# A two-layer decoder on one core: token choice by fused comparisons, and one table for the experts' results

## The chip, the cores and the metric

The kernel runs on one core of one Trainium2 chip. The time is that of one execution on the device, in microseconds (us); the kernel before was run three times. The engines of the core run their own instruction streams and wait for each other through semaphores: TensorE (PE; its weight loads are PEld), VectorE (DVE), ScalarE (ACT), GpSimd (POOL) and SyncE (SP), which issues most transfers.

## The reference

Six sublayers work on x of 8 x 256 tokens with 512 features, each followed by a layer norm of x plus its result: sparse attention, a recurrence, a mixture of experts, causal attention, cross attention and a feed-forward layer. The change touches the choice of tokens in the first, and how results come together in the third.

```python
importance = (x @ Wi + bi)[..., 0]
sorted_desc = jnp.sort(importance, axis=-1)[:, ::-1]
tidx = min(max(1, int(S * SPARSITY_THRESHOLD)), S - 1)      # 51 of 256
sparse_mask = (importance > sorted_desc[:, tidx][:, None]).astype(x.dtype)
_, top_idx = jax.lax.top_k(importance, min(MIN_TOKENS, S))  # 32
min_mask = jnp.zeros_like(importance).at[rows, top_idx].set(1.0)
sparse_mask = jnp.maximum(sparse_mask, min_mask)            # masks k and v
...
probs = jax.nn.softmax(x @ gate_w.T, axis=-1)               # 16 experts
vals, idx = jax.lax.top_k(probs, K)                         # K = 4
w = vals / jnp.sum(vals, axis=-1, keepdims=True)
combine = jnp.einsum('tke,tk->te', jax.nn.one_hot(idx, E, dtype=x.dtype), w)
act = swiglu(jnp.einsum('th,ehi->eti', x, w_gu))
y_e = jnp.einsum('eti,eih->eth', act, w_d)
out = jnp.einsum('te,eth->th', combine, y_e)
out = out + swiglu(x @ w_shared_gate_up) @ w_shared_down
x = _layernorm(x + out, axis=-1)
```

## The kernel before

The residual x stays on the chip for the whole program, as `g.xt` (the trace's `residual`): features on the partitions, 4 x 128 of them, and 2048 tokens in the free dimension. The work is cut into stages, each an `nc.Block()`; between two blocks all engines meet at a barrier, so no engine begins a stage before the last one has ended the stage ahead of it. Inside a stage the order on each engine is that of the code, and semaphores tie the engines together. The helper `Chain` (called `step`) puts a semaphore wait behind an instruction.

Token choice (`sparse_select`, lines 314 to 340). TensorE writes the importance of all tokens to every partition, ScalarE copies it to `imp`. A partition stands for token i of each half batch; `own` is that token's importance for the 16 half batches. VectorE compares all 256 importances of the batch with `own`, once with "at least" (`ge`) and once with "more" (`gt`), sums both, and counts the ties that stand earlier by the table `tri`. `n_ge` decides the threshold, `n_gt` plus the earlier ties is the token's place among the kept ones. From both comes the selection matrix `sel`, with which TensorE gathers the chosen tokens (line 377 on).

Mixture. `route` finds each token's four experts and gives every pair of token and expert a slot in tiles of 256 slots of one expert; a tile is two halves of 128. It writes the tokens' rows, scaled by 64 and split in two 16-bit parts, to the table `token_rows` in HBM, and the scaled rows in 32 bits to the second of two tables `mixed_rows`. Slots without a token point to spare rows behind the 2048 (the constant `spare`, lines 97 and 1067). `experts` runs 8 tiles of the shared expert, whose results SyncE stores into the first table (line 1210), and then 47 tiles of routed ones. For these GpSimd gathers the rows by index (line 1240) and scatters each tile's results with an addition in HBM (line 1252), the first half of a tile into the first table and the second half into the second, so that the residual is already in the sum. A tile's scatter waits until both of the tile before it have landed:

```python
def scatter(j):
    u = j % 2
    wait_out(pool, j - 1)
```

`combine` loads both tables in groups of four blocks of 128 tokens, VectorE adds them, TensorE turns each block by four transposes into one of four PSUM tiles, and ScalarE writes it back to the residual, divided by 64. Layer norm 2 follows (`layer_norm`, line 154 its first matmuls).

Of the kernel before, what the change touches and what calls it, by code (L numbers as in the profile page):

```python
# [17 lines left out]
P = 128  # L18
# [34 lines left out]
           ("choose", 17 * 17), ("spare", 1), ("half16", 2), ("nib_shift", 1)]  # L53
# [13 lines left out]
def constants():  # L67
# [29 lines left out]
    put("spare", T + 1 + p[:, None])  # L97
# [135 lines left out]
def sparse_select(nc, g, a):  # L233


    with ExitStack() as ctx:
# [15 lines left out]
        ge = sb("ge", [P, B, 2, S])  # L252
        gt = sb("gt", [P, B, 2, S])
# [55 lines left out]
        def _(dve):  # L309
# [3 lines left out]
            dve.tensor_copy(wib[:, :, :], bc(wi[:, :], 2, [P, C, P])).then_inc(wib_ready, 1)  # L313
            dve.wait_ge(imp_copied, NT)
# [4 lines left out]
            own_v = own[:, :].rearrange("p (b q) -> p b q", q=2)  # L319
            for q in range(2):  # L320
                mine = bc(own_v[:, :, q], 2, [P, B, S])
                dve.tensor_tensor(ge[:, :, q, :], imp[:, :, :], mine, ALU.is_ge)
                last = dve.tensor_tensor(gt[:, :, q, :], imp[:, :, :], mine, ALU.is_gt)
            step(last)
            n_ge, n_gt, ties, keep = (small[:, k, :] for k in range(4))
            dve.tensor_reduce(n_ge, ge[:, :, :, :].rearrange("p b q j -> p (b q) j"), AX.X, ALU.add)
            step(dve.tensor_reduce(n_gt, gt[:, :, :, :].rearrange("p b q j -> p (b q) j"), AX.X, ALU.add))

            step(dve.tensor_tensor(ge[:, :, :, :], ge[:, :, :, :], gt[:, :, :, :], ALU.subtract))
            step(dve.tensor_tensor(ge[:, :, :, :].rearrange("p b q j -> p b (q j)"),  # L330
                                   ge[:, :, :, :].rearrange("p b q j -> p b (q j)"),
                                   bc(g.const("tri"), 1, [P, B, 2 * S]), ALU.mult))
            step(dve.tensor_reduce(ties, ge[:, :, :, :].rearrange("p b q j -> p (b q) j"), AX.X, ALU.add))
            step(dve.tensor_tensor(ties, ties, n_gt, ALU.add))
# [533 lines left out]
def route(nc, g, a):  # L868
# [3 lines left out]
    with ExitStack() as ctx:  # L872
# [45 lines left out]
        def _(sp):  # L918
# [4 lines left out]
            sp.dma_start(g.rows_dram[T:T + P, :], a["one_row"][:, 0:ROW].to_broadcast([P, ROW])).then_inc(stored, 16)  # L923
            for part in g.sum_dram:
                sp.dma_start(part[T:T + P, :], a["one_row"][:, 0:D].to_broadcast([P, D])).then_inc(stored, 16)
# [536 lines left out]


def combine(nc, g):


    NTOK, GROUP = T // P, 4
    with ExitStack() as ctx:
# [1257 lines left out]
```

## Time and profile before

| | |
|---|---|
| median of 3 runs | 2708.68 us (2708.18 to 2710.73) |
| the profiled execution | 2711.14 us |
| its span | 2709.3 us |
| mean granted TensorE clock | 0.893 |
| token choice on VectorE | 41.98 to 73.07 us |
| combination, first load to last write of the residual | 1410.22 to 1439.55 us |

Times in the rows below are counted from the span's start. "Idle before" is how long the engine stood still ahead of an instruction, with what ended it. The clock is a share of 2.4 GHz. A matmul in 32 bits has more than one record.

### The profile page before, as it was taken

The page shows a single profiled execution, that of the slowest core. Times are in us where ns is not written, and L with a number is a line of the kernel's source. Part 1 is how long each engine was busy: PE and PEld are TensorE (multiplying, and loading weights), DVE is VectorE, ACT ScalarE, POOL GpSimd, SP SyncE. Part 2 cuts the span into 40 slices and gives each one's busy share as a digit, 9 for nine tenths or more (in the row PEclk, how much of TensorE's full clock was granted, in tenths as well). Part 3 has the DMA queues.
Part 4 walks back from the last instruction along what each step waited for, and adds up shares of the span by engine and source line. Part 5 has one row for each costly group of instructions (what it writes and reads, how often), then busy time and mean ns, then how long its engine had stood idle before and what let it go on. Part 6 is the DMA issues. An engine that isn't in the chain of part 4 may idle for free. (4 is left out here: it accounts for less than half of the span.)

```text
span 2709.3 us, 33393 instructions
## 1 busy us (share of the span) xinstructions
PE 2043.6 (75%) x12168; PEld 1270.0 (47%) x12203; DVE 1814.1 (67%) x2409; ACT 1326.7 (49%) x2139; POOL 953.4 (35%) x547
## 2 busy tenths in 40 slices
PE   2788765126498898988956899997994776789986
PEld 1456642012366666666633566663552332344442
DVE  4349883875776777777744356654443897999975
ACT  0013232655376776766734223323553885556656
POOL 1014443213245777777735122224111000443330
PEclk7888887668699999999987999998997998899998
DMA  3224655001637999999964000002334530000001
GB/s 141 62 93 159 241 189 221 0 0 44 235 102 246 254 251 262 247 261 256 251 152 169 0 1 1 1 1 109 92 80 140 187 118 1 0 1 1 1 0 62
DMA packets 123684, 313.63 MB, mean 116 GB/s; under 512 B 29569, under 2 KB 49537, under 8 KB 119810
## 3 DMA queue, kind: packets, MB, share of 16 engines
q1 hardware_dynamic: 102466, 260.69, 27.8%
q0 software_dynamic: 21056, 50.84, 9.5%
q8 instruction: 96, 1.57, 0.2%
q14 instruction: 66, 0.54, 0.1%
HBM read 219.59 MB, written 92.68 MB: 115 GB/s over the span
## 5 line engine op out<-in xcount | busy, mean ns | idle before, releaser
L1406 DVE SCALAR_TENSOR_TENSOR x_part<-x_group,x_scale,x_part 128x256 f32<-128x256 f32 x660 | 287.9, 477 | 144.2 <-ACT x_part L1348 137.5
L1295 PE MATMUL x_group<-x_xt,x_gu 128*128 128x256 f16 x2640 | 346.2, 275 | 2.1 <-ACT x_part L1348 1.2
L1348 ACT ACTIVATE x_part<-x_group,x_scale 128x256 f32<-128x256 f32 x660 | 276.1, 471 | 123.5 <-PE x_group L1295 117.5
L1261 POOL TENSOR_TENSOR x_part<-x_part 128x512 f32<-128x512 f32 x165 | 235.4, 1431 | 196.7 <-DVE x_part L1406 196.7
L1295 PEld LDWEIGHTS x_group<-x_xt,x_gu 128*128 128x128 fp8e4 x2640 | 237.0, 98 | 85.9 <-issue 32.4
L1312 PE MATMUL x_y_ps<-x_d_hi,x_h_hi 128*128 128x512 f32 x330 | 160.0, 485 | 68.8 <-DVE x_h_lo L1419 66.8
L2418 POOL TENSOR_TENSOR f_part<-f_part 128x1024 f32<-128x1024 f32 x44 | 120.4, 2737 | 188.0 <-DVE f_part L2445 188.0
L154 PE MATMUL mean_n<-residual,const_tables 128*128 128x512 f32 x160 | 79.3, 648 | 138.6 <-PEq L733 103.5
L1754 POOL TENSOR_TENSOR c_pt<-c_pt,const_tables 128x1024 f32<-128x1024 f32 x32 | 75.8, 2369 | 258.4 <-ACT c_pt L1728 258.4
L2316 PE MATMUL f_group<-f_x_hi,f_raw 128*128 128x512 f16 x352 | 138.9, 394 | 32.1 <-DVE f_part L2445 24.6
L1252 POOL DMA_INDIRECT mixed_rows<-x_y,moe_rows x94 | 150.1, 1597 | 31.0 <-issue 20.8
L2182 ACT ACTIVATE z_pt<-z_s 128x1024 f32<-128x1024 f32 x128 | 119.7, 1052 | 51.5 <-PE z_s L2153 50.4
L2445 DVE SCALAR_TENSOR_TENSOR f_part<-f_group,f_scale,f_part 128x512 f32<-128x512 f32 x176 | 123.9, 742 | 26.8 <-ACT f_part L2367 21.1
L2316 PE MATMUL f_group<-f_x_lo,f_raw 128*128 128x512 f16 x352 | 138.0, 392 | 0.0
L2367 ACT ACTIVATE f_part<-f_group,f_scale 128x512 f32<-128x512 f32 x176 | 111.0, 679 | 44.2 <-PE f_group L2316 44.0
L1312 PE MATMUL x_y_ps<-x_d_lo,x_h_hi 128*128 128x512 f32 x330 | 131.1, 397 | 0.0
L1312 PE MATMUL x_y_ps<-x_d_hi,x_h_lo 128*128 128x512 f32 x330 | 130.2, 395 | 0.0
L154 PEld LDWEIGHTS mean_n<-residual,const_tables 128*128 128x128 f32 x160 | 32.9, 209 | 181.6 <-issue 181.6
L1240 POOL DMA_INDIRECT x_row<-token_rows,moe_rows x94 | 102.5, 1091 | 21.5 <-issue 16.4
L1312 PEld LDWEIGHTS x_y_ps<-x_d_hi,x_h_hi 128*128 128x128 f32 x330 | 62.5, 189 | 98.0 <-DVE x_h_lo L1419 92.8
L199 ACT ACTIVATE squares_n<-centred_n 128x2048 f32<-128x2048 f32 x24 | 45.9, 1911 | 127.5 <-DVE centred_n L177 127.5
L2330 PE MATMUL f_y<-f_h_hi,f_w_hi 128*128 128x512 f32 x176 | 104.9, 596 | 3.2 <-DVE f_h_lo L2457 2.2
(331 smaller groups left out, 5042.3 us busy)
## 6 DMA issues: line engine op xcount, KB each, us to landing
x_d_hi<-down_hi SPq DMA_DIRECT2D x50, 768.0 KB, 5.7
x_d_lo<-down_lo SPq DMA_DIRECT2D x50, 768.0 KB, 5.9
x_gu<-codes_gu SPq DMA_DIRECT2D x50, 384.0 KB, 5.7
p_w<-d_s SPq DMA_DIRECT2D x17, 768.0 KB, 7.7
down_hi<-p_hi SPq DMA_DIRECT2D x17, 768.0 KB, 3.9
down_lo<-p_lo SPq DMA_DIRECT2D x17, 768.0 KB, 6.3
aux<-ct SPq DMA_DIRECT2D x2, 4096.0 KB, 16.3
cross_values<-y_v_out SPq DMA_DIRECT2D x16, 512.0 KB, 3.0
```

What stands on the lines that cost most here:

```text
L154: mm = pe.matmul(mean_ps[t % 2][:, :], g.const("mean"), tile(src, t)[:, c, :], start=c == 0, stop=c == C - 1)
L1252: pool.indirect_dma_start(out=g.sum_dram[k], out_offset=bass.IndirectOffsetOnAxis(ap=g.rows[:, at:at + 1], axis=0), in_=y[u][:, k, :], in_ ...
L1261: pool.tensor_tensor(x[:, 0, :, :], x[:, 0, :, :], x[:, 1, :, :], ALU.add).then_inc(summed, 1)
L1295: mm = pe.matmul(group_ps[s % 2][:, q, :], codes[:, q, col:col + P], xt[u][:, k, q, :], start=k == 0, stop=k == 1)
L1312: mm = pe.matmul(y_ps[half][:, :], x[u][:, k, rows], w[v][:, k, :], start=k == 0 and i == 0, stop=k == G_I - 1 and i == 2)
L1348: act.activation(part[n % PARTS][:, q, o % 2, :], group_ps[s % 2][:, q, :], ACT.Copy, scale=scale[v][:, o, q:q + 1]).then_inc(ev_act, 1)
L1406: dve.scalar_tensor_tensor(x, group_ps[s % 2][:, 2 + q, :], scale[v][:, o, 2 + q:3 + q], x, ALU.mult, ALU.add).then_inc(ev_dve, 1)
L2182: act.activation(pt[n % RING_P][:, :, :, :], s_ps[n % 3][:, :, :, :], ACT.Exp, scale=HDX ** -0.5)\
L2316: mm = pe.matmul(group_ps[c][:, :], codes[:, n, C * k + c, :], x[t % 2][:, c, :], start=i == 0, stop=i == 1)
L2367: act.activation(part[N % PARTS][:, c, k, :], group_ps[c][:, :], ACT.Copy, scale=scale[:, N % G_F, k, c:c + 1]).then_inc(ev_act, 1)
L2418: pool.tensor_tensor(x[:, 0, :, :], x[:, 0, :, :], x[:, 1, :, :], ALU.add).then_inc(summed, 1)
L2445: dve.scalar_tensor_tensor(x, group_ps[c][:, :], scale[:, N % G_F, k, c:c + 1], x, ALU.mult, ALU.add)\
```

## The change

Token choice: the two long comparisons for each half, the two sums, the subtraction, the multiplication with `tri` and the third sum are replaced by three fused instructions for each of the 16 half batches. Each compares 256 importances with the partition's own one, multiplies by a row of ones, by `tri` (earlier tokens) or by the new table `later` (the others), and writes the sum of the result with `accum_out`. "At least" among the earlier plus "more" among the later is the same place as before. The products go to 16-bit buffers that nothing reads.

Mixture: there is one table `mixed_rows`, with 256 spare rows, 128 for each half of a tile. The scaled rows are no longer stored to HBM. `combine` loads one table in eight groups of two blocks, TensorE waits for the loads directly, and VectorE multiplies the turned block by 1/64 and adds the residual that is on the chip.

VectorE at the token choice, before (`s_small` are the sums, `s_own` the own importances):

```order
L318 TENSOR_REDUCE s_own<-s_sel 128x16
L322 TENSOR_TENSOR s_ge<-s_imp,s_own 128x8x256
L323 TENSOR_TENSOR s_gt<-s_imp,s_own 128x8x256
L322 TENSOR_TENSOR s_ge<-s_imp,s_own 128x8x256
L323 TENSOR_TENSOR s_gt<-s_imp,s_own 128x8x256
L326 TENSOR_REDUCE s_small<-s_ge 128x16
L327 TENSOR_REDUCE s_small<-s_gt 128x16
L329 TENSOR_TENSOR s_ge<-s_ge,s_gt 128x4096
L330 TENSOR_TENSOR s_ge<-s_ge,const_tables 128x4096
L333 TENSOR_REDUCE s_small<-s_ge 128x16
L334 TENSOR_TENSOR s_small<-s_small 128x16
L335 TENSOR_SCALAR s_small<-s_small 128x16
```

and now:

```order
L318 TENSOR_TENSOR s_sel<-s_imp,const_tables 128x2048
L320 TENSOR_REDUCE s_own<-s_sel 128x16
L326 SCALAR_TENSOR_TENSOR s_ge,s_small<-s_imp,s_own,const_tables 128x256
L328 SCALAR_TENSOR_TENSOR s_gt,s_small<-s_imp,s_own,const_tables 128x256
L330 SCALAR_TENSOR_TENSOR s_gt,s_small<-s_imp,s_own,s_later 128x256
...
L330 SCALAR_TENSOR_TENSOR s_gt,s_small<-s_imp,s_own,s_later 128x256
L333 TENSOR_TENSOR s_small<-s_small 128x16
L334 TENSOR_SCALAR s_small<-s_small 128x16
```

Nine instructions over 2048 or 4096 elements have become 48 over 256, three for each of 16 half batches, with no wait from the second to the last.

SyncE's loads in the combination and at the start of the layer norm stage, before (the first two and what follows them; pairs like these stand four times):

```order
L1485 DMA m_mixed<-mixed_rows 128x4x512
L1485 DMA m_kept<-mixed_rows 128x4x512
...
L1468 UNCONDITIONAL_BRANCH
L219 UNCONDITIONAL_BRANCH
L1529 DMA c_rope<-rope 128x1024
L1533 DMA c_wq<-wq 128x2048
```

and now:

```order
L1482 DMA m_mixed<-mixed_rows 128x2x512 x8
L1467 UNCONDITIONAL_BRANCH
L219 UNCONDITIONAL_BRANCH
L1517 DMA c_rope<-rope 128x1024
L1521 DMA c_wq<-wq 128x2048
```

Eight loads of 1 MB, four from each table, have become eight of half the size from one. What follows is the same.

VectorE in the combination and at the start of the layer norm behind it, before:

```order
L1492 TENSOR_TENSOR m_mixed<-m_mixed,m_kept 128x512 x16
L1468 UNCONDITIONAL_BRANCH
L173 UNCONDITIONAL_BRANCH
L177 TENSOR_TENSOR centred_n<-residual,mean_n 128x2048 x3
L190 TENSOR_TENSOR residual<-centred_n,rs_n 128x4x512
```

and now:

```order
L1500 SCALAR_TENSOR_TENSOR residual<-m_turn,residual 128x4x128 x16
L1467 UNCONDITIONAL_BRANCH
L173 UNCONDITIONAL_BRANCH
L177 TENSOR_TENSOR centred_n<-residual,mean_n 128x2048 x3
L190 TENSOR_TENSOR residual<-centred_n,rs_n 128x4x512
```

The additions ahead of the transposes are gone; what ScalarE wrote behind them, VectorE now writes with the residual added.

```diff
@@ the tables of constants
-           ("choose", 17 * 17), ("spare", 1), ("half16", 2), ("nib_shift", 1)]
+           ("choose", 17 * 17), ("spare", HALVES), ("half16", 2), ("nib_shift", 1)]
-    put("spare", T + 1 + p[:, None])
+    put("spare", T + 1 + p[:, None] + P * np.arange(HALVES)[None, :])
@@ sparse_select
-        ge = sb("ge", [P, B, 2, S])
-        gt = sb("gt", [P, B, 2, S])
+        ge = sb("ge", [P, 2 * B, S], F16)
+        gt = sb("gt", [P, 2, 2 * B, S], F16)
+        later = sb("later", [P, 2 * S])
...
+            dve.tensor_scalar(later[:, :], g.const("tri"), -1.0, 1.0, ALU.mult, ALU.add)
             dve.wait_ge(imp_copied, NT)
...
-            own_v = own[:, :].rearrange("p (b q) -> p b q", q=2)
-            for q in range(2):
-                mine = bc(own_v[:, :, q], 2, [P, B, S])
-                dve.tensor_tensor(ge[:, :, q, :], imp[:, :, :], mine, ALU.is_ge)
-                last = dve.tensor_tensor(gt[:, :, q, :], imp[:, :, :], mine, ALU.is_gt)
+            n_ge, ties, after, keep = (small[:, k, :] for k in range(4))
+            ones = g.const("ones")[:, 0:1].to_broadcast([P, S])
+            for n in range(2 * B):
+                b, q, mine = n // 2, n % 2, own[:, n:n + 1]
+                earlier = g.const("tri")[:, q * S:(q + 1) * S]
+                dve.scalar_tensor_tensor(ge[:, n, :], imp[:, b, :], mine, ones, ALU.is_ge, ALU.mult,
+                                         accum_out=n_ge[:, n:n + 1])
+                dve.scalar_tensor_tensor(gt[:, 0, n, :], imp[:, b, :], mine, earlier, ALU.is_ge, ALU.mult,
+                                         accum_out=ties[:, n:n + 1])
+                last = dve.scalar_tensor_tensor(gt[:, 1, n, :], imp[:, b, :], mine, later[:, q * S:(q + 1) * S],
+                                                ALU.is_gt, ALU.mult, accum_out=after[:, n:n + 1])
             step(last)
-            n_ge, n_gt, ties, keep = (small[:, k, :] for k in range(4))
-            dve.tensor_reduce(n_ge, ge[:, :, :, :].rearrange("p b q j -> p (b q) j"), AX.X, ALU.add)
-            step(dve.tensor_reduce(n_gt, gt[:, :, :, :].rearrange("p b q j -> p (b q) j"), AX.X, ALU.add))
-
-            step(dve.tensor_tensor(ge[:, :, :, :], ge[:, :, :, :], gt[:, :, :, :], ALU.subtract))
-            step(dve.tensor_tensor(ge[:, :, :, :].rearrange("p b q j -> p b (q j)"),
-                                   ge[:, :, :, :].rearrange("p b q j -> p b (q j)"),
-                                   bc(g.const("tri"), 1, [P, B, 2 * S]), ALU.mult))
-            step(dve.tensor_reduce(ties, ge[:, :, :, :].rearrange("p b q j -> p (b q) j"), AX.X, ALU.add))
-            step(dve.tensor_tensor(ties, ties, n_gt, ALU.add))
+            step(dve.tensor_tensor(ties, ties, after, ALU.add))
@@ route, SyncE
-            sp.dma_start(g.rows_dram[T:T + P, :], a["one_row"][:, 0:ROW].to_broadcast([P, ROW])).then_inc(stored, 16)
-            for part in g.sum_dram:
-                sp.dma_start(part[T:T + P, :], a["one_row"][:, 0:D].to_broadcast([P, D])).then_inc(stored, 16)
-            kept = g.sum_dram[1][0:T, :].rearrange("(n p) f -> p n f", p=P)
+            for k in range(HALVES):
+                spare = slice(T + k * P, T + (k + 1) * P)
+                sp.dma_start(g.rows_dram[spare, :], a["one_row"][:, 0:ROW].to_broadcast([P, ROW])).then_inc(stored, 16)
+                sp.dma_start(g.sum_dram[spare, :], a["one_row"][:, 0:D].to_broadcast([P, D])).then_inc(stored, 16)
...
-                sp.dma_start(kept[:, n:n + 4, :], scaled[:, n:n + 4, :]).then_inc(stored, 16)
@@ route, VectorE
-            step(dve.tensor_scalar(empty[:, :], row_ps, 0.0, g.const("spare"), ALU.is_equal, ALU.mult))
+            for k in range(HALVES):
+                last = dve.tensor_scalar(empty[:, k::HALVES], row_ps[:, k::HALVES], 0.0, g.const("spare")[:, k:k + 1],
+                                         ALU.is_equal, ALU.mult)
+            step(last)
@@ experts: store() on SyncE, scatter() on GpSimd
-                sp.dma_start(g.sum_dram[0][j * M:(j + 1) * M, :].rearrange("(h p) f -> p h f", p=P), y[u][:, :, :])\
+                sp.dma_start(g.sum_dram[j * M:(j + 1) * M, :].rearrange("(h p) f -> p h f", p=P), y[u][:, :, :])\
...
-                    pool.indirect_dma_start(out=g.sum_dram[k], out_offset=bass.IndirectOffsetOnAxis(ap=g.rows[:, at:at + 1], axis=0),
+                    pool.indirect_dma_start(out=g.sum_dram, out_offset=bass.IndirectOffsetOnAxis(ap=g.rows[:, at:at + 1], axis=0),
@@ combine
-    NTOK, GROUP = T // P, 4
+    NTOK, GROUP = T // P, 2
...
-                for dst, src in ((mixed, g.sum_dram[0]), (kept, g.sum_dram[1])):
-                    rows = src[0:T, :].rearrange("(n p) f -> p n f", p=P)
-                    sp.dma_start(dst[:, part, :], rows[:, part, :]).then_inc(s, 16)
...
-                dve.tensor_tensor(mixed[:, n, :], mixed[:, n, :], kept[:, n, :], ALU.add).then_inc(summed, 1)
+                sp.dma_start(mixed[:, part, :], rows[:, part, :]).then_inc(s, 16)
...
             for n in range(NTOK):
-                pe.wait_ge(summed, n + 1)
+                if n % GROUP == 0:
+                    pe.wait_ge(landed[n // GROUP], 16)
                 if n >= 4:
                     pe.wait_ge(out, n - 3)
...
-        @block.scalar
-        def _(act):
+        @block.vector
+        def _(dve):
             for n in range(NTOK):
-                act.wait_ge(turned, n + 1)
-                act.activation(g.xt[:, :, n * P:(n + 1) * P], turn_ps[n % 4][:, :, :], ACT.Copy, scale=1.0 / X_GAIN)\
-                   .then_inc(out, 1)
+                x = g.xt[:, :, n * P:(n + 1) * P]
+                dve.wait_ge(turned, n + 1)
+                dve.scalar_tensor_tensor(x, turn_ps[n % 4][:, :, :], 1.0 / X_GAIN, x, ALU.mult, ALU.add).then_inc(out, 1)
@@ decoder
-        g.rows_dram = scratch("token_rows", [T + P, ROW])
+        g.rows_dram = scratch("token_rows", [T + HALVES * P, ROW])
-        g.sum_dram = [scratch(f"mixed_rows{k}", [T + P, D]) for k in range(HALVES)]
+        g.sum_dram = scratch("mixed_rows", [T + HALVES * P, D])
```

## Rows read from the trace of the kernel before

**Rows 1.** The page's first part: busy us, share of the span, instructions.
```profile
PE 2043.6 (75%) x12168; PEld 1270.0 (47%) x12203; DVE 1814.1 (67%) x2409; ACT 1326.7 (49%) x2139; POOL 953.4 (35%) x547
```

**Rows 2.** Timeline of VectorE, token choice: start us, us, instruction, idle before and releaser.
```profile
37.34 2.29 DVE L316 TENSOR_TENSOR s_sel<-s_imp,const_tables 128x2048 f32<-128x2048 f32 x1 [17.52 <-ACT s_imp L299]
...
41.98 2.29 DVE L322 TENSOR_TENSOR s_ge<-s_imp,s_own 128x2048 f32<-128x2048 f32 x1
44.19 2.28 DVE L323 TENSOR_TENSOR s_gt<-s_imp,s_own 128x2048 f32<-128x2048 f32 x1
...
50.91 4.42 DVE L326 TENSOR_REDUCE s_small<-s_ge 128x16 f32<-128x4096 f32 x1
...
73.07 0.17 DVE L334 TENSOR_TENSOR s_small<-s_small 128x16 f32<-128x16 f32 x1
73.28 0.17 DVE L335 TENSOR_SCALAR s_small<-s_small 128x16 f32<-128x16 f32 x1
73.36 0.17 DVE L336 TENSOR_SCALAR s_small<-s_small 128x16 f32<-128x16 f32 x1
```

**Rows 3.** Timeline of TensorE where the selection is ready.
```profile
78.44 6.14 PE L377 MATMUL s_row<-s_sel,const_tables 128*128 128x512 f32 x8 [41.86 <-DVE s_sel L340]
```

**Rows 4.** Timeline of the combination stage, all engines.
```profile
1410.22 0.38 SPq L1485 DMA_DIRECT2D m_mixed<-mixed_rows  x1
...
1418.44 2.50 DVE L1492 TENSOR_TENSOR m_mixed<-m_mixed,m_kept 128x512 f32<-128x512 f32 x4 [24.42 <-DMA m_kept<-mixed_rows]
...
1419.19 3.67 PE L1501 MATMUL m_turn<-const_tables,m_mixed 128*128 128x128 f32 x16 [25.95 <-DVE m_mixed L1492]
1420.34 0.60 ACT L1508 ACTIVATE residual<-m_turn 128x512 f32<-128x512 f32 x1 [27.73 <-PE m_turn L1501]
...
1421.19 0.60 ACT L1508 ACTIVATE residual<-m_turn 128x512 f32<-128x512 f32 x1 [0.26 <-PE m_turn L1501]
...
1434.80 2.50 DVE L1492 TENSOR_TENSOR m_mixed<-m_mixed,m_kept 128x512 f32<-128x512 f32 x4 [2.89 <-DMA m_kept<-mixed_rows]
...
1438.41 1.14 ACT L1508 ACTIVATE residual<-m_turn 128x512 f32<-128x512 f32 x2 [0.26 <-PE m_turn L1501]
...
1439.86 7.11 PE L154 MATMUL mean_n<-residual,const_tables 128*128 128x512 f32 x16 [0.94 <-PEq L1468]
```

**Rows 5.** Windows there: busy by engine (instructions), TensorE clock, DMA share, GB/s.
```profile
1418.00:1419.00 1.00, 0.00 (x0) 0.00 (x0) 0.56 (x1) 0.00 (x0) 0.00 (x0) 0.50 1.01 381
```

**Rows 6.** Timeline of the end of the routing stage.
```profile
688.79 1.35 SPq L935 DMA_DIRECT2D token_rows<-r_shares  x1
...
714.70 0.32 DVE L1067 TENSOR_SCALAR r_empty<-r_tok,const_tables 128x94 f32<-128x94 f32 x1 [3.08 <-PE r_tok L965]
```

**Rows 7.** Instructions by line and shape: count, busy us, mean ns, idle before.
```profile
L2445 DVE SCALAR_TENSOR_TENSOR f_part<-f_group,f_scale,f_part 128x512 f32<-128x512 f32 x176 | 123.9, 742 | 26.8 <-ACT f_part L2367 21.1 <-PE f_group L2316 5.2 <-issue 0.2
...
L829 DVE SCALAR_TENSOR_TENSOR w_e<-w_e,w_e_first,w_bb 128x1020 f32<-128x1020 f32 x8 | 10.0, 1250 | 0.0
...
L1009 DVE TENSOR_TENSOR r_p<-r_p,r_m 128x256 f32<-128x256 f32 x1 | 0.4, 426 | 0.0
```

**Rows 8.** Window just after the selection, the same columns as rows 5.
```profile
83.00:84.00 1.00, 1.00 (x4) 0.41 (x3) 0.00 (x0) 0.00 (x0) 0.00 (x0) 0.81 0.00 0
```

**Rows 9.** Timeline of TensorE in the routing stage, four transposes of the residual.
```profile
661.92 0.63 PE L955 MATMUL r_x<-const_tables,residual 128*128 128x128 f32 x4 [0.35 <-ACT r_rows L974]
```

**Rows 10.** Timeline of TensorE at the start of the last layer norm.
```profile
2665.34 9.75 PE L154 MATMUL mean_n<-aux,const_tables 128*128 128x512 f32 x16 [10.10 <-PEq L2483]
```

**Rows 11.** Timeline of GpSimd, scatters of two tiles that follow each other.
```profile
1154.85 1.62 POOL L1252 DMA_INDIRECT mixed_rows<-x_y,moe_rows  x1 [0.15 <-issue]
1156.77 1.57 POOL L1252 DMA_INDIRECT mixed_rows<-x_y,moe_rows  x1 [0.31 <-issue]
...
1166.91 1.63 POOL L1252 DMA_INDIRECT mixed_rows<-x_y,moe_rows  x1 [0.15 <-issue]
```

**Rows 12.** DMA issues between 860 and 1390 us: count, us to landing.
```profile
mixed_rows<-x_y,moe_rows POOLq DMA_INDIRECT x88, 5.4
```

More of the change, by code:

```diff
@@ L932, in _ @@
                   .then_inc(stored, 16)
-                sp.dma_start(kept[:, n:n + 4, :], scaled[:, n:n + 4, :]).then_inc(stored, 16)
             sp.wait_ge(shares_ready, 2)
             sp.dma_start(out[:, :, D:ROW], shares[:, :, :]).then_inc(stored, 16)
-            sp.wait_ge(stored, 16 * (NTOK // 2 + 4))
+            sp.wait_ge(stored, 16 * (NTOK // 4 + 2 * HALVES + 1))
         @block.tensor
@@ L1472, in combine @@
         mixed = ctx.enter_context(nc.sbuf_tensor("m_mixed", [P, NTOK, D], F32))
-        kept = ctx.enter_context(nc.sbuf_tensor("m_kept", [P, NTOK, D], F32))
         turn_ps = [ctx.enter_context(nc.psum_tensor(f"m_turn{i}", [P, C, P], F32)) for i in range(4)]
         landed = [sem(f"landed{i}") for i in range(NTOK // GROUP)]
-        summed, turned, out = sem("summed"), sem("turned"), sem("out")
+        turned, out = sem("turned"), sem("out")
         block = ctx.enter_context(nc.Block())
@@ L1480, in _ @@
         def _(sp):
+            rows = g.sum_dram[0:T, :].rearrange("(n p) f -> p n f", p=P)
             for i, s in enumerate(landed):
                 part = slice(i * GROUP, (i + 1) * GROUP)
-                for dst, src in ((mixed, g.sum_dram[0]), (kept, g.sum_dram[1])):
-                    rows = src[0:T, :].rearrange("(n p) f -> p n f", p=P)
-                    sp.dma_start(dst[:, part, :], rows[:, part, :]).then_inc(s, 16)
-        @block.vector
-        def _(dve):
-            for n in range(NTOK):
-                if n % GROUP == 0:
-                    dve.wait_ge(landed[n // GROUP], 32)
-                dve.tensor_tensor(mixed[:, n, :], mixed[:, n, :], kept[:, n, :], ALU.add).then_inc(summed, 1)
+                sp.dma_start(mixed[:, part, :], rows[:, part, :]).then_inc(s, 16)
         @block.tensor
@@ L1502, in _ @@
                 mm.then_inc(turned, 1)
-        @block.scalar
-        def _(act):
+        @block.vector
+        def _(dve):
             for n in range(NTOK):
-                act.wait_ge(turned, n + 1)
-                act.activation(g.xt[:, :, n * P:(n + 1) * P], turn_ps[n % 4][:, :, :], ACT.Copy, scale=1.0 / X_GAIN)\
-                   .then_inc(out, 1)
-X_RING = 16
+                x = g.xt[:, :, n * P:(n + 1) * P]
+                dve.wait_ge(turned, n + 1)
+                dve.scalar_tensor_tensor(x, turn_ps[n % 4][:, :, :], 1.0 / X_GAIN, x, ALU.mult, ALU.add).then_inc(out, 1)
 def causal_weights(nc, g, a, ctx):
```

## The prediction

> **What bounds the kernel now.** I read the page first: its busy shares [rows 1] say only that no engine is full over the span, and they average over stages that barriers separate. A stage ends when its last engine ends. So a saving on the path inside one stage moves all that follows by the same amount, and one that lies beside that path is worth nothing. I then read the timeline of the stages that the change touches.
>
> Token choice. VectorE works without a gap from 41.98 to 73.07 us: four comparisons over 2048 elements, then five passes over 4096, of which the first stands in the rows [rows 2]. TensorE has nothing to do meanwhile; its next matmul comes after 41.86 us of waiting for the selection [rows 3]. These 73.07 - 41.98 = 31.1 us are all on the path.
>
> Combination of the experts' results. SyncE issues the first load at 1410.22, VectorE starts at 1418.44, its last four additions at 1434.80, when the last load has landed; ScalarE ends at 1438.41 + 1.14 = 1439.55, and the next stage's first matmul is at 1439.86 [rows 4]. Meanwhile the DMA engines move 381 GB/s [rows 5]. The eight loads bring 8 x 128 x 4 x 512 x 4 bytes = 8.39 MB, 22.0 us at that rate; from first issue to last landing it took 24.6, so start and receipt cost 2.6 us. Transfer bounds this stage, with 4.75 us of tail behind the last landing.
>
> Routing. Its last store is issued at 688.79; VectorE makes the row numbers at 714.70 [rows 6]. The stores are over long before, and VectorE's chain is the path there.
>
> **Token choice: the sum.** Removed is every instruction in the 31.1 us. In their place stand 48 fused comparisons over 256 elements, each with an accumulated sum, back to back; the only wait stands behind the last. The trace has no instruction with an accumulated sum, so I bound it.
> The main part first. 2048 elements last 2.29 us and 4096 last 4.42, so an element costs 1.04 ns. Two long comparisons without a wait start 2.21 us apart [rows 2], which is 2.13 for the elements and 0.08 for a start: neighbours overlap by 0.08. So 256 elements come to 0.27 + 0.08 = 0.35 us from start to start. An instruction of that size lasts 0.426 [rows 7], less 0.08 the same.
> Then the sum has to be written. Nearest is a tiny instruction: 0.08 us without a wait (73.28 to 73.36), 0.21 with one (73.07 to 73.28), 0.17 long [rows 2].
> Lower end: the write costs nothing, 48 x 0.35 = 16.8 us. Upper end: both parts run each for themselves, 0.43 + 0.17 = 0.60, 28.8 us. I take the unwaited tiny instruction, as these are unwaited too: 0.43 us each, 48 x 0.43 = 20.6, with the last one's tail 20.8 us. Saved 31.1 - 20.8 = 10.3 us, between 14.3 and 2.3.
> The new table of later positions, one pass over 512 elements, runs while VectorE waits 17.52 us for the importance scores [rows 2]: nothing. Without that cover it would cost some 0.6 us. Results in 16 bits change nothing that I can see, since the inputs stay at 32.
> The Trainium skill, page "VectorE: DVE Perf Modes", section "Two Vector instructions with no wait between them", says that an instruction which also writes out its accumulator is two, the main one and an accumulator read. With the 58 cycles plus one per element at 0.96 GHz of that page's errata section, the 48 would take 48 x (0.327 + 0.061) = 18.6 us, an estimate from that page. Its section "The DRAIN you can't avoid" speaks against the change: the next operation is not to start before the pipe has emptied, and one should minimise the number of operations, which here rises from nine to 48. The trace has an overlap of 0.08 us against it for plain instructions, and nothing for accumulated ones; if it held there, rival B would be the outcome.
>
> **Routing: the sum.** Four 1 MB stores of the scaled rows go, and one small store more is issued at the stage's start. All of it ends well before 714.70 [rows 6], so this gives nothing. Had SyncE's queue been last, the four would give back some 2.7 us each (1 MB at 381 GB/s); the times exclude it. The step that marks empty slots is split into two halves of 47 columns: one start more, 0.1 us on the path.
>
> **Experts: the sum.** The same bytes are scattered behind the same waits, into one table instead of two. I put it at nothing; rival E says what it could cost.
>
> **Combination: the sum.** Half the bytes, in eight pieces of 0.52 MB, which take 1.38 us each at 381 GB/s. With 2.7 us of start and receipt (the first pair's landing at 1418.44 less 5.5 us of transfer gives the same) the first piece lands at 1410.22 + 2.7 + 1.38 = 1414.3 and the last at 1410.22 + 2.7 + 11.0 = 1423.9. TensorE now waits for the landing itself. From its first transpose to the engine behind it are 1.15 us (1419.19 to 1420.34), and the next block follows 0.85 later (1421.19) [rows 4], at clock 0.50, which is 1.2 GHz [rows 5]. Blocks land 0.69 us apart, so TensorE bounds at first. After the long wait in token choice its clock came back within 83 to 84 us, 4.7 to 5.6 us behind the matmul of 78.44 [rows 3, 8]; I take the same here, about 1419.5. Four transposes at 2.4 GHz take 0.63 us in all [rows 9], and VectorE becomes the bound. It scales and adds the residual in one fused instruction over 512 elements out of PSUM; the nearest lasts 0.742 [rows 7], 0.66 from start to start with the 0.08 of overlap.
> Block 1 reaches VectorE at 1415.45; five more at 0.85 make 1419.7, ten at 0.66 make 1426.3 for the last start, and its 0.74 end at 1427.0. The last landing is 3 us earlier and no longer the limit. Saved 1439.55 - 1427.0 = 12.5 us. With the clock at 1.2 GHz throughout it is 1415.45 + 15 x 0.85 + 0.74 = 1428.9, saved 10.6. With VectorE as the only limit it is 1415.45 + 15 x 0.66 + 0.74 = 1426.1, saved 13.5. ScalarE's 16 evictions go, but were late only by the transposes' pace. Late next is VectorE's own pace.
>
> **Sum.** 10.3 - 0.1 + 12.5 = 22.7 us. The profiled execution took 2711.14 us, with a span of 2709.3 and 1.8 around it; less 22.7 gives 2688.4 for one like it. The median of the runs is 2.46 us below the profiled one, so I predict 2686.0 us.
>
> **Rivals.**
> B, slow accumulation. Writing the sum empties the pipe 48 times: 28.8 us, 2.3 saved there, 14.7 in all, 2694.0. For it: a waited tiny instruction costs 0.21 us, and this form may behave like a waited one. Against it: plain neighbours overlap.
> C, half rate. The fused form with two 32-bit sources in SBUF takes two cycles an element when it accumulates: 0.35 + 0.27 + 0.08 = 0.70, 33.6 us for the 48. This part then loses 2.5 us, and the whole saves 9.9: 2698.8. Against it: a fused instruction with such sources over 1020 elements lasts 1.25 us, one cycle an element, though without a sum [rows 7]. The skill's "Vector Engine (DVE) Microarchitecture Reference", section "Points that are easy to get wrong", has this rule: two non-bf16 SBUF sources halve this form's throughput. The trace disagrees for the plain form.
> D, clock. TensorE stays at 1.2 GHz through the combination, and is there still when the layer norm starts. The 16 matmul records that follow took 7.11 us now [rows 4], and 9.75 at the start of the last layer norm [rows 10], 2.6 more. With 1.9 in the combination that is 4.5 us, 2690.5. Against it: the clock was back by the layer norm's start though TensorE worked with pauses before it.
> E, slower: the scatters wait for each other. A tile's two scatters start at 1154.85 and 1156.77, the next tile's at 1166.91, and these wait for the former [rows 11]. A scatter lands 5.4 us after its issue [rows 12], at 1162.2, so 4.7 us are to spare. If in the shared table the second had to stand behind the first's accumulation and took twice 5.4 us, it would land at 1167.6, 0.7 us late, and 46 tiles would lose 30 us or so: 2716. It decides from 0.5 us a tile on (46 x 0.5 = 23). Against it: the halves hold different tokens and get separate spare rows, and two scatters to two tables passed through the same queue.
> Smaller: the constant table grows from 2256 to 2257 columns, so what is allocated behind it moves. The trace has only one layout; I allow 2 us either way.
>
> **How the numbers follow.** The forecast as summed has 0.58, B 0.20, C 0.06, D 0.10, E 0.03, and the lower ends together (14.3 and 13.5, which make 2681.0) 0.03. A measurement of this kernel tells some 0.2% from no change, 5.4 us. Faster by more than that are all but E and the worst mixtures: 0.95. Within it: 0.02, a weak E or C with D. Slower: 0.03, E. The range goes from 2678 (lower ends and 2 us of layout, and one more for the bounds' rounding) to 2697 (B with part of D); C and E are left out.
>
> **What would show it.** 48 fused comparisons, the first near 42.0 and the tiny addition behind them near 62.8; near 71 it is B, beyond 74 it is C. In the combination, counted from its first load's issue: first transpose after 4.1 us, clock at 1.0 after 9 to 10, last VectorE end after 16.8; two more if the clock doesn't rise. The next layer norm's first 16 matmul records in 7.1 us, or the clock had fallen. The experts' stage the same within 2 us, or it is E or the layout. Routing the same to 0.3 us. A saving under 10 us or over 32 would say that I read the wrong path.

## The result and the profile after

The changed kernel takes 2683.47 us, the median of 3 runs (2681.58 to 2684.53), against 2708.68 before: a ratio of 0.9904 with a 95% interval of [0.9882, 0.9926], 25.2 us less. The forecast was 2686.0. The profiled execution took 2683.47 us with a span of 2681.7; the profiled one of before took 2711.14, so the two traces are 27.7 us apart, 2.5 more than the medians.

VectorE in the token choice, first and last fused instructions (timeline: start us, us long, instruction, idle before):

```profile
37.31 2.29 DVE L318 TENSOR_TENSOR s_sel<-s_imp,const_tables 128x2048 f32<-128x2048 f32 x1 [16.71 <-ACT s_imp L300]
...
41.96 0.49 DVE L326 SCALAR_TENSOR_TENSOR s_ge<-s_imp,s_own,const_tables 128x256 f16<-128x256 f32 x1
42.37 0.08 DVE L326 DVE_READ_ACCUMULATOR s_ge<-s_imp,s_own,const_tables 128x1 f32 x1
42.37 0.48 DVE L328 SCALAR_TENSOR_TENSOR s_gt<-s_imp,s_own,const_tables 128x256 f16<-128x256 f32 x1
42.77 0.08 DVE L328 DVE_READ_ACCUMULATOR s_gt<-s_imp,s_own,const_tables 128x1 f32 x1
42.77 0.48 DVE L330 SCALAR_TENSOR_TENSOR s_gt<-s_imp,s_own,s_later 128x256 f16<-128x256 f32 x1
...
61.05 0.48 DVE L330 SCALAR_TENSOR_TENSOR s_gt<-s_imp,s_own,s_later 128x256 f16<-128x256 f32 x1
61.46 0.08 DVE L330 DVE_READ_ACCUMULATOR s_gt<-s_imp,s_own,s_later 128x1 f32 x1
61.57 0.18 DVE L333 TENSOR_TENSOR s_small<-s_small 128x16 f32<-128x16 f32 x1
```

The first comparison starts where it started before [rows 2], the tiny addition at 61.57 instead of 73.07. So 31.1 us have become 61.57 - 41.96 = 19.6, which saves 11.5. Every fused instruction brings a read of its sum as a row of its own (`DVE_READ_ACCUMULATOR`), 0.08 us long; but the next comparison starts in the same moment as the read. From start to start it is (61.05 - 41.96) / 47 = 0.406 us.

The combination, all engines but the weight loads:

```profile
1400.41 4.00 SPq L1482 DMA_DIRECT2D m_mixed<-mixed_rows  x8
...
1404.10 5.23 PE L1492 MATMUL m_turn<-const_tables,m_mixed 128*128 128x128 f32 x32 [20.04 <-DMA m_mixed<-mixed_rows]
1405.25 0.69 DVE L1500 SCALAR_TENSOR_TENSOR residual<-m_turn,residual 128x512 f32<-128x512 f32 x1 [20.40 <-PE m_turn L1492]
1406.10 0.69 DVE L1500 SCALAR_TENSOR_TENSOR residual<-m_turn,residual 128x512 f32<-128x512 f32 x1 [0.16 <-PE m_turn L1492]
1406.95 8.57 DVE L1500 SCALAR_TENSOR_TENSOR residual<-m_turn,residual 128x512 f32<-128x512 f32 x14 [0.16 <-PE m_turn L1492]
...
1412.23 1.09 PE L1492 MATMUL m_turn<-const_tables,m_mixed 128*128 128x128 f32 x8 [0.26 <-DMA m_mixed<-mixed_rows]
...
1413.54 1.09 PE L1492 MATMUL m_turn<-const_tables,m_mixed 128*128 128x128 f32 x8 [0.22 <-DMA m_mixed<-mixed_rows]
```

Read against [rows 4]: from the first load's issue at 1400.41 to VectorE's end at 1406.95 + 8.57 = 1415.52 are 15.1 us, where it was 29.3. That saves 14.2. (Each transpose is one record here, four to a block, 64 in all.) VectorE follows TensorE at 0.85 us a block for two steps, and then runs 14 blocks without a gap, 0.61 us apart. The last four pairs of blocks wait some 0.2 us for their load, and VectorE ends 2.0 us after the last pair's transposes begin at 1413.54, so the landings are all but level with VectorE at the end.

Windows of the same stretch (busy of PE, PEld, DVE, ACT, POOL; then clock, DMA share, GB/s):

```profile
1406.00:1407.00 1.00, 1.00 (x7) 1.00 (x6) 0.74 (x2) 0.00 (x0) 0.00 (x0) 0.50 1.04 377
1407.00:1408.00 1.00, 1.00 (x10) 1.00 (x9) 1.00 (x2) 0.00 (x0) 0.00 (x0) 0.88 1.04 387
1408.00:1409.00 1.00, 1.00 (x12) 1.00 (x10) 1.00 (x3) 0.00 (x0) 0.00 (x0) 1.00 1.07 397
```

TensorE's clock came from 0.50 (1.2 GHz) to 1.00 (2.4 GHz) at about 1407.2 (a mean of 0.88 over the microsecond from 1407), 3.1 us after its first transpose; in that microsecond VectorE goes from 0.74 busy to 1.00.

The layer norm behind it begins with 16 records in 7.11 us at full clock, as in [rows 4]. The experts' stage is 674.9 us from its first matmul to its last, 673.7 before, and 691.3 to the combination's first load, 690.7 before; a scatter still lands 5.3 us after its issue (5.4 in [rows 12]). Up to layer norm 2 the traces are 24.0 us apart (1439.86 against 1415.85), from the last layer norm on 27.5 (2665.34 and 2637.82). The 3.5 us between, most of them in the causal attention (352.6 us before from TensorE's first projection to its last, 349.7 after), stand where nothing was changed. A second trace of the changed kernel (`after_again`, below) does not have them: it is 26.2 us ahead at layer norm 2 and 26.7 at the last one. They are spread between executions of the same code.

### The profile page after: what moved, and what is told of

Read it like the earlier page. It is cut to its first block and busy times, and to the rows that moved or that the text cites. A ratio compares the mean times of both kernels' runs of the same rounds, so it can differ in the third digit from the quotient of the medians.

```text
span 2681.7 us, 33457 instructions
## 1 busy us (share of the span) xinstructions
PE 2044.9 (76%) x12168; PEld 1269.5 (47%) x12203; DVE 1802.0 (67%) x2498; ACT 1316.9 (49%) x2123; POOL 954.0 (36%) x547
## 3 DMA queue, kind: packets, MB, share of 16 engines
q1 hardware_dynamic: 98450, 252.58, 26.7%
```

## The experiments

e1 to e4 ran as one set with common runs of the kernel before; e5, e6, e7 and e9 as a second; e8, the changed kernel again and e10 as a third; e11 by itself.

**One part of the change alone.** `e1_choice_only` is the kernel before with the new lines of `sparse_select`; `e2_table_only` is the changed kernel with the old ones.

```diff
 e1: before, with in sparse_select
-    dve.tensor_tensor(ge..., ALU.is_ge) ... tensor_reduce(ties, ...)      (nine long instructions)
+    dve.scalar_tensor_tensor(..., accum_out=...)                          (48 fused ones, table `later`)
 e2: after, with the same lines turned back
```

> The kernel before with the fused token choice alone; two tables, row stores and the combination stay. Theory 1 (each part saves what its own stage shows, the parts add up, and the rest of the difference between the two profiled executions is the spread of one kernel's own executions): about 11.3 us faster than before (31.1 less 19.5), ratio 0.9958, and the combination stage of 29.3 us unchanged. Rival 2 (the earlier or later start of stages, or the layout, gives several us more elsewhere, since the profiled executions differ by 27.6 and not by 25.7): 13 us or more faster. Rival 3 (part of the gain at the choice is given back in the attention stage behind it, where the difference fell from 11.1 to 8.9 us): 9 us or less.

> The changed kernel with the old token choice: one table, no row stores, the residual added on the chip. Theory 1: about 14.2 us faster than before (29.3 less 15.1 in the combination), ratio 0.9948; routing and experts the same within 1 us. Rival 2: 17 us or more, with the surplus in stages that this part does not touch. Rival E of the prediction (scatters into one table wait for each other): the experts' stage longer than before's, by more than 2 us.

Measured: e1 2699.1 us, ratio 0.9960 [0.9946, 0.9973], 10.7 us less than the 2709.79 of before in that set; e2 2696.57 us, ratio 0.9947 [0.9933, 0.9960], 13.2 less. Together 23.9, against 25.2 for the whole change; each of these differences is known to some 4 us. The rows are sharper, and agree: in e1 the stretch from first comparison to tiny addition is as short as in the changed kernel, and e2's combination lasts 15.3 us from issue to end, with scatters that begin and end where those of before do. The parts add up as far as these times can tell, and neither hides the other.

**Layout.** `e3_wide_table` is the kernel before with the constant table one column wider, as the change makes it.

```diff
-           ("choose", 17 * 17), ("spare", 1), ("half16", 2), ("nib_shift", 1)]
+           ("choose", 17 * 17), ("spare", 2), ("half16", 2), ("nib_shift", 1)]
...
-            step(dve.tensor_scalar(empty[:, :], row_ps, 0.0, g.const("spare"), ALU.is_equal, ALU.mult))
+            step(dve.tensor_scalar(empty[:, :], row_ps, 0.0, g.const("spare")[:, 0:1], ALU.is_equal, ALU.mult))
```

> The kernel before with nothing but the constant table one column wider (the second column of spare is not read), so that everything allocated behind it on the chip lies 32 bytes further. Theory 1: the layout does nothing, within 1 us of before, and its profiled execution shows how far two executions of practically the same kernel differ stage by stage (1 to 3 us in the first attention and in the causal attention). Rival 2: 2 us or more faster than before, the layout being what the two parts' sum leaves over.

Measured: 2709.88 us, ratio 1.0002 [0.9993, 1.0011]. This one shift of what lies behind the table costs nothing that can be told (the interval reaches from 1.9 us less to 3.0 more); the 2 us of the prediction were not needed.

**The stores of the scaled rows.** `e4_row_stores_back` gives the changed kernel its four 1 MB stores again, to a table that nothing reads.

```diff
+            kept = g.unused_dram.rearrange("(n p) f -> p n f", p=P)
...
+                sp.dma_start(kept[:, n:n + 4, :], scaled[:, n:n + 4, :]).then_inc(stored, 16)
```

> The changed kernel with the four 1 MB stores of the scaled rows put back in the routing stage, into a table that nothing reads. Theory 1: they lie beside VectorE's chain there, so the time is that of the changed kernel, 2683.5 within 1 us, and the routing stage keeps its 79.5 us from TensorE's first to last matmul. Rival: they held up the engines (by the DMA traffic on the chip's memory or by SyncE), then 2 to 10 us more than the changed kernel, in the routing stage.

Measured: 2684.68 us, ratio 0.9911 [0.9896, 0.9926], 1.2 above the changed kernel's first median and 0.5 below its second. SyncE's queue and VectorE's row numbers in e4:

```profile
674.13 0.36 SPq L930 DMA_DIRECT2D token_rows<-r_rows  x1
674.53 1.35 SPq L933 DMA_DIRECT2D unused_rows<-r_scaled  x1
675.93 1.31 SPq L935 DMA_DIRECT2D token_rows<-r_shares  x1
...
701.86 0.44 DVE L1068 TENSOR_SCALAR r_empty<-r_tok,const_tables 128x47 f32<-128x47 f32 x2 [3.08 <-PE r_tok L965]
```

The issue of the last store ends 24.6 us ahead of the instruction that ends this part of the routing. It waits 3.08 us for TensorE, as before [rows 6], and for no transfer. The stores are off the path.

**The bytes of the combination.** `e5_loads_twice` loads each piece twice, so that 8.39 MB move again, with the new order of work.

```diff
+        again = ctx.enter_context(nc.sbuf_tensor("m_again", [P, NTOK, D], F32))
...
-                sp.dma_start(mixed[:, part, :], rows[:, part, :]).then_inc(s, 16)
+                for dst in (again, mixed):
+                    sp.dma_start(dst[:, part, :], rows[:, part, :]).then_inc(s, 16)
...
-                    pe.wait_ge(landed[n // GROUP], 16)
+                    pe.wait_ge(landed[n // GROUP], 32)
```

> The changed kernel, whose combination loads every piece twice, the first time into a buffer that nothing reads, so that 8.39 MB move again as before the change, with everything behind the loads as changed. Theory 1 (transfer bounds the combination, and halving its bytes is what the table change gives): 10.9 us more in that stage, 26 us instead of 15.1, and 2694.4 in all. Rival (the gain came from the shorter chain per block, without the addition ahead of the transposes and without ScalarE): under 3 us more, 18 us or less for the stage.

Measured: 2695.83 us, ratio 0.9952 [0.9936, 0.9969], 12.4 above the changed kernel's first median and 10.7 above its second. The stage takes from 1399.37 to 1426.54, 27.2 us. Its timeline in the middle and at the start of the layer norm:

```profile
1415.76 1.97 PE L1494 MATMUL m_turn<-const_tables,m_mixed 128*128 128x128 f32 x8 [0.74 <-DMA m_mixed<-mixed_rows]
...
1418.47 1.97 PE L1494 MATMUL m_turn<-const_tables,m_mixed 128*128 128x128 f32 x8 [0.74 <-DMA m_mixed<-mixed_rows]
...
1425.85 0.69 DVE L1502 SCALAR_TENSOR_TENSOR residual<-m_turn,residual 128x512 f32<-128x512 f32 x1 [0.16 <-PE m_turn L1494]
...
1426.86 5.32 PE L154 MATMUL mean_n<-residual,const_tables 128*128 128x512 f32 x8 [1.05 <-PEq L1467]
```

A pair of blocks comes every 2.71 us instead of 1.35, which is 1.05 MB at 387 GB/s, and TensorE waits 0.74 us for each. So 12.1 of the 14.2 us saved here come with the halved bytes. The other 2.1 are the tail: one fused instruction behind the last transposes in place of four additions ahead of them and a ScalarE write each. It also shows what rival D looked for: TensorE pauses each time, its clock stays at 0.50 to the end, a pair takes 1.97 us, and the layer norm starts at 1.2 GHz (its first 16 records take 8.76 us, not 7.11). The changed kernel pauses too, but by 0.2 us and at full clock.

**The sums.** `e6_no_sums` is the changed kernel without `accum_out`. The counts are set to zero beforehand, so the real choice of tokens is left out.

```diff
+            step(dve.memset(small[:, :, :], 0.0))
...
-                dve.scalar_tensor_tensor(ge[:, n, :], imp[:, b, :], mine, ones, ALU.is_ge, ALU.mult,
-                                         accum_out=n_ge[:, n:n + 1])
+                dve.scalar_tensor_tensor(ge[:, n, :], imp[:, b, :], mine, ones, ALU.is_ge, ALU.mult)
...
```

> The changed kernel whose 48 fused comparisons write no accumulated sums (the counts are set to zero beforehand, so the choice of tokens is left out; the instructions behind it stay). Theory 1 (the accumulator's read costs 0.06 to 0.08 us on the path, the main part 0.35): the comparisons start 0.34 to 0.35 us apart instead of 0.407, the 48 take 16.5 us instead of 19.5. Rival (the fused instruction itself is dearer than a plain one, its row says 0.48 us against 0.43, and the read is hidden behind it): 0.40 us apart as with the sums. In both cases 3 us or less of the total, which one look does not tell, so the profile decides.

Measured in one run: 2685.53 us, with a span of 2683.7; the rows decide here, since 0.5 us can't be told by the time. VectorE, first three and last:

```profile
40.85 0.48 DVE L327 SCALAR_TENSOR_TENSOR s_ge<-s_imp,s_own,const_tables 128x256 f16<-128x256 f32 x1
41.25 0.48 DVE L328 SCALAR_TENSOR_TENSOR s_gt<-s_imp,s_own,const_tables 128x256 f16<-128x256 f32 x1
41.65 0.48 DVE L329 SCALAR_TENSOR_TENSOR s_gt<-s_imp,s_own,s_later 128x256 f16<-128x256 f32 x1
...
59.46 0.48 DVE L329 SCALAR_TENSOR_TENSOR s_gt<-s_imp,s_own,s_later 128x256 f16<-128x256 f32 x1
```

(59.46 - 40.85) / 47 = 0.396 us from start to start, against 0.406 with the sums. The sum costs 0.01 us an instruction, 0.5 us in all. What is dearer than I took it for is the fused instruction itself: 0.48 us long, where the plain one of that size took 0.426 [rows 7].

**The size of the pieces.** `e7_pieces_of_4` and `e8_pieces_of_1` change one number; `after_again` is the changed kernel beside e8.

```diff
-    NTOK, GROUP = T // P, 2
+    NTOK, GROUP = T // P, 4        (e8: 1)
```

> The changed kernel with four loads of 1 MB in the combination instead of eight of 0.5 MB. Theory 1: the last byte comes at the same time, but the first transpose starts 1.4 us later (5.1 us after the first issue instead of 3.7) and four blocks instead of two stand behind the last landing, so the stage takes 16.5 us instead of 15.1 and the total 1.4 us more than the changed kernel's. Rival (the size of the pieces is what set the pace): 3 us or more.

> The changed kernel with its combination loaded in sixteen pieces of 0.26 MB instead of eight of 0.52. Theory: once TensorE's clock is back the landings are the bound, so what counts is the last landing. The bytes are the same and the last landing moves only by what is behind it: one block instead of two, some 0.6 us. The first piece lands 0.7 us earlier. Pieces of 1 MB measured 17.3 us for the stage against 15.1, that is 2.2 more for a doubled piece; halved again it should give about 14.2, and the whole 0.5 to 1 us less than the changed kernel beside it. Rival: each load costs SyncE an issue of some 0.5 us, and 16 of them take 8 us, which still fits beside 11 us of transfer; if smaller pieces moved at a lower rate, the stage would be 15.1 or longer.

> The changed kernel itself, on the same chip as the two others, so that they can be compared with it directly. Both theories: 0.9904 of the kernel before, as measured first, and the same stages: token choice 19.5 us, combination 15.1 us.

Measured: e7 2685.84 us, ratio 0.9912 [0.9895, 0.9928]; e8 2684.89, 0.9908 [0.9891, 0.9924]; the changed kernel again 2685.13, 0.9909 [0.9893, 0.9926]. The times say no more than that these are the same; the stages say more. Issue to VectorE's end is 17.3 us in e7, 15.2 in the changed kernel again, and 1414.57 - 1397.72 = 16.9 in e8, where I expected 14.2. That was wrong. The rows of e8:

```profile
1397.72 8.58 SPq L1482 DMA_DIRECT2D m_mixed<-mixed_rows  x16
1400.34 1.97 PE L1492 MATMUL m_turn<-const_tables,m_mixed 128*128 128x128 f32 x8 [20.38 <-DMA m_mixed<-mixed_rows]
...
1402.87 1.12 PE L1492 MATMUL m_turn<-const_tables,m_mixed 128*128 128x128 f32 x4 [0.56 <-DMA m_mixed<-mixed_rows]
...
1404.75 8.63 PE L1492 MATMUL m_turn<-const_tables,m_mixed 128*128 128x128 f32 x52 [0.77 <-DMA m_mixed<-mixed_rows]
```

and two of its windows:

```profile
1401.00:1402.00 1.00, 1.00 (x7) 0.91 (x5) 0.51 (x1) 0.00 (x0) 0.00 (x0) 0.50 1.02 223
...
1408.00:1409.00 1.00, 1.00 (x9) 1.00 (x8) 0.84 (x2) 0.00 (x0) 0.00 (x0) 0.66 1.06 404
```

The first piece lands 1.1 us earlier, but small pieces move more slowly at first (223 GB/s in that microsecond, and 309 to 371 around it), TensorE pauses twice at half clock, and the full clock comes only 8.3 us after the first transpose. Until then a block takes 0.85 us. That the pauses are what delays the clock is not shown: it came 6.1 us after the first transpose in e6, whose combination has pairs and in which TensorE did not pause once, and 4.9 us after it in e9, with single blocks and one pause.

**A version that beats both.** In `e9_scalar_counts` ScalarE, idle there, counts the tokens of lesser importance in two passes (Relu of own minus importance, then Sign with its sum), which replaces the first of the three fused instructions, 16 of 48. The combination has pieces of one block. `e10_scalar_counts_again` is the same kernel beside the changed one and e8; `e11_scalar_counts_pairs` has pieces of two blocks.

```diff
+            for n in range(2 * B):
+                mm = act.activation(below[:, n, :], imp[:, n // 2, :], ACT.Relu, bias=own[:, n:n + 1], scale=-1.0)
...
+            for n in range(2 * B):
+                mm = act.activation(below[:, n, :], below[:, n, :], ACT.Sign, accum_out=n_less[:, n:n + 1])
...
-                dve.scalar_tensor_tensor(ge[:, n, :], imp[:, b, :], mine, ones, ALU.is_ge, ALU.mult,
-                                         accum_out=n_ge[:, n:n + 1])
...
-            dve.tensor_scalar(n_ge, n_ge, float(KEEP) + 0.5, None, ALU.is_lt)
+            dve.wait_ge(less_ready, 1)
+            dve.tensor_scalar(n_ge, n_less[:, :], S - float(KEEP) - 0.5, None, ALU.is_gt)
```

> The changed kernel with one third of the comparisons moved: ScalarE, which idles there, counts the tokens with less importance (a Relu of the difference for each of 16 half batches, then a Sign of each with an accumulated sum), VectorE keeps the 32 others; and the combination loads pieces of one block. Theory 1: VectorE's 32 take 13.0 us instead of 19.5; ScalarE's 32 passes take 0.40 us each plus the accumulator's read, 13 to 17 us, so the end of the choice comes 2.5 to 6.5 us earlier; the pieces give 0.5 us; 2677 to 2681 in all. Rival (ScalarE's read of an accumulator is dear, 0.2 us and more each with the pipe emptied, and a new function table has to be loaded): ScalarE takes 20 us or more and nothing is won, 2683 or later.

> The kernel with the counts of lesser tokens on ScalarE and single blocks in the combination, again, beside the changed kernel. Theory: 16 of the 48 comparisons off VectorE are worth 16 x 0.407 = 6.5 us on the path, less what the wait for own costs, and about 1 us in the combination: 6 to 7 us below the changed kernel's stages, if nothing behind gives it back. The first run was only 3.2 us below, on another chip. Rival: the stages behind (attention, causal) give half of it back through VectorE and GpSimd, in every run, and the difference is 3 us here too.

> ScalarE counts the lesser tokens as in the two runs before, and the combination is loaded in eight pieces of 0.52 MB again instead of sixteen of 0.26. Theory: small pieces cost time here, since TensorE pauses between them while its clock is at 1.2 GHz and gets the full clock only 5.8 to 8 us after its first transpose, against 2.5 to 3 us with pairs; the stages were 15.4, 15.7 and 16.9 us with single blocks and 15.1 to 15.2 with pairs. So this combination is 15.1 us, token choice 12.3 to 13.1 us, and the whole 0.3 to 0.6 us below the run with single blocks, 0.9885 of the kernel before; by time alone that is inside what a measurement can tell, the stage's rows must show it. Rival: the clock comes back late here too (over 5 us), and the stage is 16 us or more; then the size of the pieces is not what sets it.

Measured: e9 2680.25 us, ratio 0.9891 [0.9875, 0.9908]; e10 2678.77, 0.9887 [0.9870, 0.9903]; e11 2678.86, 0.9886 [0.9869, 0.9902]. Beside e10 the changed kernel took 2685.13: 6.4 us more, and the runs don't overlap (2678.67 to 2679.98 against 2684.27 to 2685.40). ScalarE works beside VectorE and ends about when it does. ScalarE in e10 first, then VectorE in e11:

```profile
41.27 6.49 ACT L306 ACTIVATE s_xsel<-s_imp,s_own 128x256 f32<-128x256 f32 x16 [4.74 <-DVE s_own L330]
47.80 0.42 ACT L310 ACTIVATE s_xsel<-s_xsel 128x256 f32<-128x256 f32 x1
48.12 0.19 ACT L310 ACTIVATION_READ_ACCUMULATOR s_xsel<-s_xsel 128x1 f32 x1
48.21 0.40 ACT L310 ACTIVATE s_xsel<-s_xsel 128x256 f32<-128x256 f32 x1
```

```profile
41.47 0.48 DVE L336 SCALAR_TENSOR_TENSOR s_gt<-s_imp,s_own,const_tables 128x256 f16<-128x256 f32 x1
...
54.59 0.17 DVE L341 TENSOR_TENSOR s_small<-s_small 128x16 f32<-128x16 f32 x1
54.80 0.17 DVE L343 TENSOR_SCALAR s_small<-s_n_less 128x16 f32<-128x16 f32 x1
```

The choice is 54.59 - 41.47 = 13.1 us instead of 19.6, so 6.5 of it is the 16 instructions. For the pieces I was wrong again: e11's combination takes 15.7 us like e10's (15.7; e9's 15.4), and not 15.1. Its pieces are pairs and TensorE doesn't pause, but the clock comes back 5.0 us after the first transpose, where it took 3.1 and 2.7 in the two traces of the changed kernel. So the size of the pieces is not all that sets it; with the same combination, six traces have it back after 2.7, 3.1, 3.1 (e2), 4.3 (e4), 5.0 (e11) and 6.1 us (e6), with 15.1 to 16.1 us for the stage, and what decides that stays open. Single blocks took 15.4, 15.7 and 16.9, so a loss by small pieces is not clear of this spread either.

## Why the prediction was right, and where its sizes were off

The mechanism was right in both places and the total is 2.5 us too cautious: the forecast saving was 22.7 us, the measured one 25.2. The rows of the stages give 11.5 - 0.1 + 14.2 = 25.6.

Token choice: right path, saving 10.3 forecast, 11.5 measured. The term was made of a main part of 0.35 us and a sum of 0.08; measured it is 0.396 and 0.01 (e6). Two errors of opposite sign made a good total: the plain instruction was a poor neighbour for the fused one, and the read's length, 0.08 as I had taken it, is not its cost, since the next instruction starts with it. The Trainium skill, page "VectorE: DVE Perf Modes", section "Two Vector instructions with no wait between them", was right that there are two instructions. The estimate from that page, 18.6 us, is 1.0 below the 19.6 measured. Its section "The DRAIN you can't avoid" has the next operation start only when the pipe is empty, unless nothing holds it; the trace shows the second case, 0.406 us from start to start with 0.48 us for each. The advice to minimise the number of operations stands in the same page's section "Rules for kernel authors" and not where the prediction puts it; here 48 took 19.6 us and nine long ones 31.1.

B, slow accumulation (0.60 us each), and C, half rate (0.70): both fell with the first rows, 0.406. The rule behind C, in the Trainium skill's "Vector Engine (DVE) Microarchitecture Reference", section "Points that are easy to get wrong", does not hold for this form with a sum either: 0.406 us for 256 elements, where C had 0.70.

Combination: 12.5 forecast, 14.2 measured, 1.7 more. By the forecast's own terms: VectorE's first start came 4.84 us after the issue, not 5.23 (0.4); the full clock came after two steps of 0.85, not five (0.6); the steps behind are 0.606, not 0.66 (13 of them, 0.7). "Late next is VectorE's own pace" was right, with the landings level beside it. That the last landing is "no longer the limit" was not: the forecast had 3.1 us between it and VectorE's end, and the last pair's transposes waited 0.22 us for it, 2.0 us before that end. The clock's return was taken from another place of the program, 4.7 to 5.6 us; that it came after 3.1 here was luck, since it took 2.7 to 6.1 us in the six traces with this combination.

Routing: nothing, as forecast for the stores (e4); the split of the empty slots shows as 0.44 us for both halves at the stage's end against 0.32 [rows 6], the 0.1 forecast. Experts: 1.2 us longer from first matmul to last, inside the 2 us allowed, and not by the table: with two tables as before, the traces of e1 and e3 have 675.1 and 675.3, with one table e2 has 675.6, against 674.9 here. E, waiting scatters, fell: GpSimd's two scatters of a tile start 1.93 us apart as before [rows 11], and land after 5.3:

```profile
1156.50 1.63 POOL L1253 DMA_INDIRECT mixed_rows<-x_y,moe_rows  x1 [0.16 <-issue]
1158.43 1.57 POOL L1253 DMA_INDIRECT mixed_rows<-x_y,moe_rows  x1 [0.30 <-issue]
...
1168.57 1.63 POOL L1253 DMA_INDIRECT mixed_rows<-x_y,moe_rows  x1 [0.16 <-issue]
```

D, the clock: not in the two traces of the changed kernel, whose layer norm starts with 7.1 us for its 16 records. But it did not fall as a rival. e5 shows it whole, and e6, whose combination is the changed kernel's own, shows its second half:

```profile
1403.50 10.64 PE L1491 MATMUL m_turn<-const_tables,m_mixed 128*128 128x128 f32 x64 [19.90 <-DMA m_mixed<-mixed_rows]
...
1416.14 8.80 PE L154 MATMUL mean_n<-residual,const_tables 128*128 128x512 f32 x16 [2.00 <-PEq L1466]
```

The clock was back at 1409.6 and fell to 0.50 again at about 1416.4, after TensorE had stood still for 2.0 us between the stages. Against the changed kernel the late return cost 1.0 us in the stage and the fall 1.7 in the layer norm. In e7 TensorE stood still as long and kept its clock. The old combination can end so too: in e1's trace the same 16 records take 9.44 us. Layout: nothing (e3).

What stays open: in stages that the change doesn't touch, two executions of the same code differ by more than the small terms here. The two traces of the changed kernel reach the first layer norm at 444.65 and 439.85, layer norm 2 at 1415.85 and 1413.70, and the last one at 2637.82 and 2638.59. So the first is 8.9 us ahead of before (453.56) at the first layer norm and the second 13.7, with 11.5 saved in both at the token choice, and whether the attention behind it gives anything back can't be told from them. What moves those stages was not looked for.

## What to carry to other kernels

Where a count or a sum follows a comparison, try it fused: here the write of the sum was nearly free on VectorE (0.01 us), and instructions of 256 elements were long enough to pay. Take the price of a fused instruction from a fused one, and from start to start, not from its length. When loads bound a stage, halve the bytes first; pieces smaller or larger than pairs won nothing here. Then look which idle engine can take a third of the work. And before you read a cause into 1 or 2 us between two traces, take a second trace of the same kernel.

## What the runs showed of the hardware that I had not expected

- A read of VectorE's accumulator is a row of 0.08 us, and adds 0.01 us from start to start. On ScalarE it is 0.19 us long, and a pass over 256 elements with its sum starts every 0.40 us.
- The full clock came 2.7, 3.1, 3.1, 4.3, 5.0 and 6.1 us after the first transpose in six traces of the same combination, 4.5 us after it with pieces of four blocks (e7), 4.9, 6.2 and 8.3 with single blocks (e9, e10, e8), and not at all in 21.6 us with a pause of about 0.74 us ahead of each pair (e5).
- Sixteen loads of 0.26 MB moved 223 to 371 GB/s in each of the seven microseconds from 1399 to 1406 (e8, first issue at 1397.72). Eight of 0.52 MB moved 377 to 410 in each of the nine from 1403 to 1412 (changed kernel, first issue at 1400.41).
